# Softmax row sums of a small-head attention layer: GpSimd folds and VectorE with one transpose per group, in place of matmuls with ones

## The chip, the cores and the metric

One core of a Trainium2 chip runs the whole program. The metric is device time in microseconds (us), the median of several executions.

## The reference

The program is a decoder of four layers on x (8 sequences of 128 tokens, width 256), each layer a mixer, a cross block and a feed-forward block, each behind a layer norm and added to x. The change touches the mixer of layer 1 alone, an attention with 32 query heads of width 8, 8 key/value heads (one for four query heads), rotary embeddings and a causal mask:

```python
x = x + _L1_attn_ref(_layernorm(x, axis=-1), L1_attn_Wq, L1_attn_Wk, L1_attn_Wv, L1_attn_Wo)
# inside, for each sequence and each head h of 32, with kv head h // 4:
#   P = softmax(q_h @ k.T / sqrt(8) + causal mask)        (128 x 128)
#   y_h = P @ v                                           (128 x 8)
# and the 32 heads side by side times Wo
```

The kernel computes exp(score - row maximum) first, multiplies that by v, and divides by the row's sum of exponentials afterwards.

## The kernel before

All data of the stage lies in SBUF. The layer's name in the code is `l1a`; the cross block of layer 2 (`l2x`) has heads of the same size and runs through the same code, `heads`. It has a version on each engine: TensorE at L921, ScalarE near L1674, VectorE near L2358.

A **unit** `u` is four heads of one sequence: 128 queries x 4 x 128 keys, 64 units in all (UNITS). Its four jobs are:

- `("s", u)`: a mask matmul and a score matmul fill one PSUM bank (128 x 512). VectorE takes the negated row maxima (L2371), ScalarE writes four exponentials of 128 x 128 into a ring of eight slots in `work` at 12288 (L1697). The bank is free when the last of the four is written.
- `("t", u)`: TensorE transposes the four 128 x 128 blocks (L957) into a bank; ScalarE (even units, L1703) or VectorE (odd units, L2380) copies the bank into a ring of eight slots in `work` at 8192.
- `("pv", x)`, one for the four units of group `x`: TensorE multiplies by windows of v (16 matmuls) and then by windows of ones (16 matmuls), so that one bank holds the unnormalised outputs, heads times channels on the partitions and queries along the columns, and beside them the sums, in the same layout. VectorE inverts the sums (L2387) and multiplies (L2391) into XT. TensorE waits for the copies of the group's last two units.
- `("o", bp)`, for four groups: the output projection, then the residual add on VectorE (L2403) and the statistics for the next layer norm (L2040, L2043).

**The order** is a list written out by `heads_plan`, in rounds of three units. Every engine walks the same list and picks its own work. Round `r` holds the scores of units 3r to 3r+2, a `pv` if one is due (group x in round (4x+3)//3 + 2), the transposes of the round before, and an `o` if one is due. Engines run strictly in their own order.

**PSUM banks**: the function `banks` hands the eight banks to the jobs in the order of the lists, one after the other, round and round. On TensorE `begin` waits until the job that last had the bank has freed it. For a round's scores, TensorE takes all three banks before the first mask matmul:

```python
os = [begin(layer, "s", u) for u in units]
```

GpSimd does nothing in this stage but the two small square roots of the next layer norm (`roots`, L647 and L650, on halves of the sequences), which follow in its program directly on those of this layer. SyncE loads the next weights and starts the next context loads when the last job of `l1a` is full. The array C holds data of an earlier stage that is no longer read.

Of the kernel before, what the change touches and what calls it, by code (L numbers as in the profile page):

```python
# [6 lines left out]
P = 128  # L7
NB = 8
D = 256
# [146 lines left out]
def heads_plan(sums_at=None):  # L156


    l = []
    for r in range(ROUNDS + 5):  # L160
        l += [("s", u) for u in round_of(r)]
        if r == sums_at:
            l += [("ws",)]
        l += [("pv", x) for x in range(UNITS // 4) if (4 * x + 3) // 3 + 2 == r]
        l += [("t", u) for u in round_of(r - 1)]
        if sums_at is not None and r == ROUNDS + 1:
            l += [("qt", 0)]
        l += [("o", bp) for bp in range(4) if (16 * bp + 15) // 3 + 4 == r]
    return l
# [73 lines left out]
def build(nc, a, out):  # L243
# [3 lines left out]
    with ExitStack() as ctx:  # L247
# [70 lines left out]
        tables_ready, queries_out = sem("tables_ready"), Handoff("queries_out")  # L318
        halves_ready, steps_ready, rates_ready = sem("halves_ready"), sem("steps_ready"), sem("rates_ready")
        half_steps, turned, head_squares, head_roots = Handoff("half_steps"), Handoff("turned"), Handoff("head_squares"), Handoff("head_roots")  # L320
        sums_inverse, scaled_probs = Handoff("sums_inverse"), Handoff("scaled_probs")
        to_turn, key_normed, key_rooted = Handoff("to_turn"), Handoff("key_normed"), Handoff("key_rooted")
        key_squares, key_roots, scaled_keys, to_park = Handoff("key_squares"), Handoff("key_roots"), Handoff("scaled_keys"), Handoff("to_park")
# [143 lines left out]


        keys_beside = WA[:, 5200:5456]

        def l1a_k(g):

# [159 lines left out]
        def _(pool):  # L632
# [52 lines left out]
            for k, n in enumerate(("k", "ks")):  # L685
                for c in range(2):
                    nc.gpsimd.tensor_copy(r3(keys_beside[:, c * P + k * 64:c * P + k * 64 + 64], 8),
                                          W(WA, W_L1A, n, c * D, (c + 1) * D).rearrange("p (a r d) -> p a r d", r=4, d=8)[:, :, 0, :]).then_inc(tables_ready, 1)
            roots()
            roots()  # L690
            def turn(q, cos, sin):

# [155 lines left out]
        def _(pe):  # L848
# [72 lines left out]
            def heads(layer, wo, pad):  # L921

                kbd = r3(wk(0, 8 * N), N)
                for key in heads_plan(SUMS_AT if layer == "l2x" else None):
# [29 lines left out]
                    if key[0] == "t":  # L954
                        pe.wait_ge(*freed(J(layer, "s", key[1])))
                        for i in range(4):
                            ins = nc.tensor.transpose(o[:, i * P:(i + 1) * P],  # L957
                                                      wk(12288 + (key[1] % 8) * G + i * P, P), cst("ident"))
                        end(ins)
                    elif key[0] == "pv":  # L960

                        x = key[1]
                        pe.wait_ge(*freed(J(layer, "t", 4 * x + 2)))
                        pe.wait_ge(*freed(J(layer, "t", 4 * x + 3)))
                        for part in range(2):
                            for h in range(4):
                                for k in range(4):
                                    u = 4 * x + k
                                    window = v_windows[:, u * 32 + 24 - 8 * h:u * 32 + 56 - 8 * h] if part == 0 else ones_window[:, 24 - 8 * h:56 - 8 * h]
                                    ins = mm(o[32 * k:32 * k + 32, part * P:(part + 1) * P], window,  # L970
                                             wk(8192 + (u % 8) * G + h * P, P), h == 0, h == 3)
                        end(ins)
                    else:
                        bp = key[1]
                        for x in range(4):
                            pe.wait_ge(*freed(J(layer, "pv", 4 * bp + x)))
                        for i in range(2):
                            for c in range(2):
                                lo = (bp % 2) * G + (2 * i + c) * P
                                ins = mm(o[:, i * D:(i + 1) * D], XT[:, lo:lo + P],  # L980
                                         wo[:, c * D:(c + 1) * D], c == 0, c == 1)
                        end(ins)
# [539 lines left out]
        def _(act):  # L1522
# [151 lines left out]
            def heads(layer):  # L1674
                for key in heads_plan(SUMS_AT if layer == "l2x" else None):
# [16 lines left out]
                    if key[0] == "s":  # L1692
                        act.wait_ge(dve_to_act.sem, dve_to_act.next())
                        if u >= 8:
                            act.wait_ge(*full(J(layer, "t", u - 8)))
                        for h in range(4):
                            f(wk(12288 + (u % 8) * G + h * P, P), bank(j)[:, h * P:(h + 1) * P], ACT.Exp,  # L1697
                              bias=sm(704 + (u % 8) * 4 + h, 1)).then_inc(*act_step(*([j] if h == 3 else [])))
# [333 lines left out]
        def _(dve):  # L2032
# [317 lines left out]
            def hidden_evac(b):  # L2350
# [4 lines left out]
                    dve.wait_ge(*full(J("l2f", "o", b - 4)))  # L2355
                v.tensor_copy(XT[:, :].bitcast(BF16)[:, (b % 4) * 1024:(b % 4 + 1) * 1024], bank(j).bitcast(BF16)).then_inc(*dve_step(j))

            def heads(layer):  # L2358

                for key in heads_plan(SUMS_AT if layer == "l2x" else None):  # L2360
# [20 lines left out]
                    elif key[0] == "pv":  # L2381
                        x = key[1]
                        bp, lo = x // 4, (x // 4 % 2) * G + (x % 4) * P
                        j = J(layer, "pv", x)
                        dve.wait_ge(*full(j))
                        rs = wk(17920, P)
                        v.reciprocal(rs, bank(j)[:, P:2 * P]).then_inc(*dve_step())  # L2387
                        dve.wait_ge(*dve_last())
# [1 line left out]
                            dve.wait_ge(*full(J(layer, "o", bp - 2)))  # L2390
                        v.tensor_tensor(XT[:, lo:lo + P], bank(j, P, P), rs, ALU.mult).then_inc(*dve_step(j))  # L2391
                        dve.wait_ge(*dve_last())
                    elif key[0] == "ws":
                        j = J(layer, "ws")
                        dve.wait_ge(*full(j))
# [548 lines left out]
```

## Time and profile before

| | us |
|---|---|
| median of 3 runs | 1538.31 (1536.23 to 1540.87) |
| span of the profiled execution | 1538.9 |
| TensorE busy | 1388.0 (90%) |
| VectorE busy | 912.7 (59%) |
| ScalarE busy | 766.8 (50%) |
| GpSimd busy | 453.6 (29%) |
| `heads` of `l1a`, first score to last residual add | 406 to 521 |
| transposes L957, both layers | 67.1 |
| exponentials L1697, both layers | 137.7 |

Busy time is that of an engine's instructions without register, branch and semaphore work. PE is TensorE, DVE VectorE, ACT ScalarE, POOL GpSimd. An fp32 matmul leaves two records, and some records are missing: of three mask matmuls often only two are there, and such a row starts 0.2 us late. Times of the trace are counted from the start of the span.

### The profile page before, as it was taken

How to read it: one execution, taken by the hardware profiler on the slowest of the kernel's cores; microseconds unless marked ns; L12 is line 12 of the kernel's file. 1: busy time of each engine (PE TensorE's matmuls, PEld its weight loads, DVE VectorE, ACT ScalarE, POOL GpSimd, SP SyncE). 2: the span in 40 equal slices, each digit the busy share in tenths (PEclk: the TensorE clock that was granted, in tenths of full speed). 3: DMA queues.
4: the chain of work that ended last, by engine and by line, in shares of the span. 5: the costliest groups of instructions: out<-in, count | busy, mean ns of one | idle time of the engine just before them, and what ended most of it. 6: DMA issues, size and time to landing. Idle time of an engine off the chain costs nothing.

```text
span 1538.9 us, 25724 instructions
## 1 busy us (share of the span) xinstructions
PE 1388.0 (90%) x9822; PEld 880.0 (57%) x9840; DVE 912.7 (59%) x1665; ACT 766.8 (50%) x1847; POOL 453.6 (29%) x400
## 2 busy tenths in 40 slices
PE   7868999999899879999999989988996888888799
PEld 3534565555466545666666764654663545546636
DVE  6694322224578655645555787945787576575632
ACT  3362111111778567777776457448776453362230
POOL 3140000000000268886881000110924235314100
PEclk9888999999999999999999999998998788989989
DMA  8020211001200300000000100020001100000000
GB/s 255 14 96 1 67 49 44 1 0 63 102 2 2 125 0 7 8 8 7 8 8 1 76 23 1 1 82 1 3 2 71 56 0 3 3 1 3 29 1 28
DMA packets 21854, 48.12 MB, mean 31 GB/s; under 512 B 1506, under 2 KB 16995, under 8 KB 20580
## 3 DMA queue, kind: packets, MB, share of 16 engines
q1 hardware_dynamic: 21732, 46.47, 8.7%
q8 instruction: 79, 1.29, 0.4%
q14 instruction: 43, 0.35, 0.1%
HBM read 41.22 MB, written 5.24 MB: 30 GB/s over the span
## 4 chain that ended last, share of the span: by engine, by line
PE 67%; DVE 19%; ACT 6%; issue 4%; POOL 4%; DMA 0%; DVEq 0%; ACTq 0%; POOLq 0%
PE PS L862 48%; PE PS L1092 5%; DVE work L2568 4%; PE PS L1151 3%; PE PS L957 3%; PE PS L1392 2%; ACT work L1697 2%; PE PS L874 2%; PE PS L1189 2%; DVE small L2040 1%; PE PS L1421 1%; DVE work L2186 1%; DVE X L2547 1%; DVE work L2536 1%; POOL work L795 1%
## 5 line engine op out<-in xcount | busy, mean ns | idle before, releaser
L862 PE MATMUL PS<-XT,WB 128*128 128x512 f32 (+1 forms) x688 | 300.0, 594 | 5.1 <-DVE XT L2066 2.8
L862 PEld LDWEIGHTS PS<-XT,WB 128*128 128x128 f32 (+1 forms) x688 | 126.7, 190 | 149.1 <-issue 145.4
L1697 ACT ACTIVATE work<-PS,small 128x128 f32<-128x128 f32 x512 | 137.7, 416 | 45.2 <-DVE small L2371 45.2
L2261 DVE TENSOR_TENSOR work<-PS,work 128x512 f32<-128x512 f32 x48 | 33.1, 691 | 168.4 <-PE PS L862 168.4
L1625 ACT ACTIVATE work<-PS 128x512 f32<-128x512 f32 x48 | 28.7, 597 | 193.6 <-PE PS L862 193.6
L647 POOL TENSOR_SCALAR small<-small 128x4 f32<-128x4 f32 x22 | 5.0, 229 | 405.9 <-DVE small L2043 405.8
L2371 DVE TENSOR_REDUCE small<-PS 128x4 f32<-128x512 f32 x128 | 80.5, 684 | 41.2 <-PE PS L862 39.8
L862 PE MATMUL PS<-XT,WA 128*128 128x512 f32 (+2 forms) x224 | 97.7, 596 | 6.1 <-DVEq L2571 3.7
L2568 DVE SCALAR_TENSOR_TENSOR work<-PS,vec,work 128x508 f32<-128x508 f32 (+2 forms) x108 | 80.2, 742 | 14.4 <-DVE work L2568 7.2
L1092 PE MATMUL PS<-WB,work 128*128 128x256 f32 x384 | 86.9, 379 | 0.5 <-DVE work L2266 0.5
L1092 PEld LDWEIGHTS PS<-WB,work 128*128 128x128 f32 x384 | 72.8, 190 | 18.3 <-issue 7.7
L862 PE MATMUL PS<-WA,XT 128*128 128x256 f32 (+1 forms) x384 | 78.1, 362 | 3.3 <-DVE XT L2391 2.4
L862 PE MATMUL PS<-work,WA 128*32 128x128 f32 (+1 forms) x2072 | 75.5, 278 | 3.0 <-DVE work L2380 1.8
L862 PE MATMUL PS<-work 128*128 128x64 f32 (+4 forms) x368 | 73.8, 351 | 3.0 <-DVE work L2620 1.8
L862 PEld LDWEIGHTS PS<-work,WA 128*32 128x32 f32 (+1 forms) x2072 | 57.6, 111 | 32.5 <-issue 32.5
L862 PEld LDWEIGHTS PS<-WA,XT 128*128 128x128 f32 x384 | 67.5, 190 | 12.3 <-issue 4.5
L862 PEld LDWEIGHTS PS<-XT,WA 128*128 128x128 f32 (+2 forms) x224 | 39.0, 186 | 60.6 <-issue 50.1
L1544 ACT ACTIVATE XN<-X,small 128x256 f32<-128x256 f32 x44 | 24.0, 593 | 97.8 <-DVE small L2049 97.6
L874 PE MATMUL PS<-cst,XN 128*128 128x128 f32 x176 | 37.5, 372 | 35.9 <-DVE XN L2053 35.4
L957 PE MATMUL PS<-cst,work 128*128 128x128 f32 x512 | 67.1, 281 | 2.8 <-ACT work L1697 2.8
L862 PE MATMUL PS<-WB,C 128*128 128x256 f32 (+1 forms) x287 | 67.3, 379 | 0.2
L957 PEld LDWEIGHTS PS<-cst,work 128*128 128x128 f32 x512 | 56.2, 143 | 19.5 <-issue 19.5
(375 smaller groups left out, 2893.7 us busy)
## 6 DMA issues: line engine op xcount, KB each, us to landing
WB<-in_l0f SPq DMA_DIRECT2D x8, 768.0 KB, 7.6
WB<-in_l1x SPq DMA_DIRECT2D x1, 6144.0 KB, 18.2
WB<-in_l0f SPq DMA_DIRECT2D x32, 96.0 KB, 7.3
WB<-in_l2f SPq DMA_DIRECT2D x1, 3072.0 KB, 10.5
WA<-in_l3a SPq DMA_DIRECT2D x1, 2624.0 KB, 8.9
WB<-in_l3f SPq DMA_DIRECT2D x1, 2064.0 KB, 7.8
WA<-in_l1f SPq DMA_DIRECT2D x1, 2056.0 KB, 11.2
C<-in_ctx SPq DMA_DIRECT2D x2, 1024.0 KB, 7.0
```

Of the source, the lines that this page charges most:

```text
L862: mm = lambda o, l, r, s, e: nc.tensor.matmul(o, l, r, start=s, stop=e)
L874: ins = nc.tensor.transpose(o[:, i * P:(i + 1) * P], source[:, b * D + c * P:b * D + (c + 1) * P], cst("ident"))
L957: ins = nc.tensor.transpose(o[:, i * P:(i + 1) * P], wk(12288 + (key[1] % 8) * G + i * P, P), cst("ident"))
L1092: ins = nc.tensor.matmul(o[:, i * D:(i + 1) * D], l0f_h(x)[:, b * P:(b + 1) * P], quad(x // 3, "down")[:, x % 3 * D:(x % 3 + 1) * D], star ...
L1151: ins = nc.tensor.matmul(o[:, i * D:(i + 1) * D], l1x_q(t // 4, 2 * s_ + i)[:, r * P:(r + 1) * P], wk(8192 + (t // 4 % 2) * 1024 + r * D, ...
L1189: ins = nc.tensor.transpose(o[:, j * P:(j + 1) * P], l1x_p(x)[:, j * D + kc * P:j * D + (kc + 1) * P], cst("ident"))
L1392: more = lambda o, l, r, e: nc.tensor.matmul(o, l, r, start=False, stop=e, skip_group_check=True)
L1625: f(l0f_s(m)[:, g * G:(g + 1) * G], bank(j), ACT.Silu).then_inc(*act_step(j))
L1697: f(wk(12288 + (u % 8) * G + h * P, P), bank(j)[:, h * P:(h + 1) * P], ACT.Exp, bias=sm(704 + (u % 8) * 4 + h, 1)).then_inc(*act_step(*([j ...
L2261: v.tensor_tensor(l0f_h(m)[:, lo:lo + G], bank(j), l0f_s(m)[:, lo:lo + G], ALU.mult).then_inc(*dve_step(j))
L2371: v.tensor_reduce(sm(704 + (u % 8) * 4, 4), r3(bank(j), P), AX.X, ALU.max, negate=True).then_inc(*dve_step(dve_to_act))
L2568: v.scalar_tensor_tensor(d[:, :, k:P], p[:, :, 0:P - k], vec(taps[0], taps[1] + 3 - k), d[:, :, k:P], ALU.mult, ALU.add).then_inc(*dve_ste ...
```

## The change

- `heads_plan` gets a job `("rb", x)` for each group in `l1a`, one round behind the group's `pv` and ahead of a `pv` in the same round.
- GpSimd folds each unit's exponentials: the 128 columns of each of four blocks to 64 (`fold_once`), then to 32 (`fold_twice`, a ring of eight slots). The first fold of unit u waits until the unit's exponentials are written, the second for the first and, from unit 8 on, until VectorE has passed the group that used the slots.
- VectorE, at a group's `pv`: `inverse_of(x)` reduces 4 x 128 folded columns to 16 sums, inverts them, and spreads each over 8 columns (128 x 128). Then it copies the `pv` bank to XT. At `rb` it multiplies XT by the `rb` bank.
- TensorE: `pv` has only the 16 matmuls with v in this layer; `rb` is one transpose of the spread inverses into a bank. The output projection waits for `rb` in place of `pv`.
- ScalarE, from unit 8 on, waits before a unit's exponentials also for the first fold of the unit eight before, whose slot it overwrites.
- `l2x` keeps its matmuls with ones and its order.

```diff
--- before.py
+++ after.py
@@ -161,6 +161,8 @@
         l += [("s", u) for u in round_of(r)]
         if r == sums_at:
             l += [("ws",)]
+        if sums_at is None:
+            l += [("rb", x) for x in range(UNITS // 4) if (4 * x + 3) // 3 + 3 == r]
         l += [("pv", x) for x in range(UNITS // 4) if (4 * x + 3) // 3 + 2 == r]
         l += [("t", u) for u in round_of(r - 1)]
         if sums_at is not None and r == ROUNDS + 1:
@@ -318,6 +320,7 @@
         tables_ready, queries_out = sem("tables_ready"), Handoff("queries_out")
         halves_ready, steps_ready, rates_ready = sem("halves_ready"), sem("steps_ready"), sem("rates_ready")
         half_steps, turned, head_squares, head_roots = Handoff("half_steps"), Handoff("turned"), Handoff("head_squares"), Handoff("head_roots")
+        folded_once, folded_twice, inverse_sums = sem("folded_once"), sem("folded_twice"), sem("inverse_sums")
         sums_inverse, scaled_probs = Handoff("sums_inverse"), Handoff("scaled_probs")
         to_turn, key_normed, key_rooted = Handoff("to_turn"), Handoff("key_normed"), Handoff("key_rooted")
         key_squares, key_roots, scaled_keys, to_park = Handoff("key_squares"), Handoff("key_roots"), Handoff("scaled_keys"), Handoff("to_park")
@@ -467,6 +470,18 @@
 
 
         keys_beside = WA[:, 5200:5456]
+
+        def fold_once(u):
+
+            return C[:, (u % 2) * D:(u % 2 + 1) * D]
+
+        def fold_twice(u, n=1):
+
+            return C[:, 512 + (u % 8) * P:512 + (u % 8 + n) * P]
+
+        def inverse_spread(x):
+
+            return wk(17920 + (x % 2) * P, P)
 
         def l1a_k(g):
 
@@ -687,6 +702,15 @@
                     nc.gpsimd.tensor_copy(r3(keys_beside[:, c * P + k * 64:c * P + k * 64 + 64], 8),
                                           W(WA, W_L1A, n, c * D, (c + 1) * D).rearrange("p (a r d) -> p a r d", r=4, d=8)[:, :, 0, :]).then_inc(tables_ready, 1)
             roots()
+            for u in range(UNITS):
+                halves = r3(wk(12288 + (u % 8) * G, G), P)
+                pool.wait_ge(*freed(job_of[("l1a", "s", u)]))
+                nc.gpsimd.tensor_tensor(r3(fold_once(u), 64), halves[:, :, 0:64], halves[:, :, 64:P], ALU.add).then_inc(folded_once, 1)
+                pool.wait_ge(folded_once, u + 1)
+                if u >= 8:
+                    pool.wait_ge(inverse_sums, (u - 8) // 4 + 1)
+                once = r3(fold_once(u), 64)
+                nc.gpsimd.tensor_tensor(r3(fold_twice(u), 32), once[:, :, 0:32], once[:, :, 32:64], ALU.add).then_inc(folded_twice, 1)
             roots()
             def turn(q, cos, sin):
 
@@ -962,7 +986,7 @@
                         x = key[1]
                         pe.wait_ge(*freed(J(layer, "t", 4 * x + 2)))
                         pe.wait_ge(*freed(J(layer, "t", 4 * x + 3)))
-                        for part in range(2):
+                        for part in range(1 if layer == "l1a" else 2):
                             for h in range(4):
                                 for k in range(4):
                                     u = 4 * x + k
@@ -970,10 +994,13 @@
                                     ins = mm(o[32 * k:32 * k + 32, part * P:(part + 1) * P], window,
                                              wk(8192 + (u % 8) * G + h * P, P), h == 0, h == 3)
                         end(ins)
+                    elif key[0] == "rb":
+                        pe.wait_ge(inverse_sums, key[1] + 1)
+                        end(nc.tensor.transpose(o[:, 0:P], inverse_spread(key[1]), cst("ident")))
                     else:
                         bp = key[1]
                         for x in range(4):
-                            pe.wait_ge(*freed(J(layer, "pv", 4 * bp + x)))
+                            pe.wait_ge(*freed(J(layer, "rb" if layer == "l1a" else "pv", 4 * bp + x)))
                         for i in range(2):
                             for c in range(2):
                                 lo = (bp % 2) * G + (2 * i + c) * P
@@ -1693,6 +1720,8 @@
                         act.wait_ge(dve_to_act.sem, dve_to_act.next())
                         if u >= 8:
                             act.wait_ge(*full(J(layer, "t", u - 8)))
+                            if layer == "l1a":
+                                act.wait_ge(folded_once, u - 7)
                         for h in range(4):
                             f(wk(12288 + (u % 8) * G + h * P, P), bank(j)[:, h * P:(h + 1) * P], ACT.Exp,
                               bias=sm(704 + (u % 8) * 4 + h, 1)).then_inc(*act_step(*([j] if h == 3 else [])))
@@ -2355,6 +2384,18 @@
                     dve.wait_ge(*full(J("l2f", "o", b - 4)))
                 v.tensor_copy(XT[:, :].bitcast(BF16)[:, (b % 4) * 1024:(b % 4 + 1) * 1024], bank(j).bitcast(BF16)).then_inc(*dve_step(j))
 
+            def inverse_of(x):
+
+                sums, inverse = C[:, 1536:1552], C[:, 1552:1568]
+                dve.wait_ge(folded_twice, 4 * x + 4)
+                v.tensor_reduce(sums, r3(fold_twice(4 * x, 4), 32), AX.X, ALU.add).then_inc(*dve_step())
+                dve.wait_ge(*dve_last())
+                v.reciprocal(inverse, sums).then_inc(*dve_step())
+                dve.wait_ge(*dve_last())
+                if x >= 2:
+                    dve.wait_ge(*full(J("l1a", "rb", x - 2)))
+                v.tensor_copy(r3(inverse_spread(x), 8), inverse.unsqueeze(2).to_broadcast([P, 16, 8])).then_inc(inverse_sums, 1)
+
             def heads(layer):
 
                 for key in heads_plan(SUMS_AT if layer == "l2x" else None):
@@ -2382,7 +2423,14 @@
                         x = key[1]
                         bp, lo = x // 4, (x // 4 % 2) * G + (x % 4) * P
                         j = J(layer, "pv", x)
+                        if layer == "l1a":
+                            inverse_of(x)
                         dve.wait_ge(*full(j))
+                        if layer == "l1a":
+                            if bp >= 2:
+                                dve.wait_ge(*full(J(layer, "o", bp - 2)))
+                            v.tensor_copy(XT[:, lo:lo + P], bank(j, P, P)).then_inc(*dve_step(j))
+                            continue
                         rs = wk(17920, P)
                         v.reciprocal(rs, bank(j)[:, P:2 * P]).then_inc(*dve_step())
                         dve.wait_ge(*dve_last())
@@ -2390,6 +2438,13 @@
                             dve.wait_ge(*full(J(layer, "o", bp - 2)))
                         v.tensor_tensor(XT[:, lo:lo + P], bank(j, P, P), rs, ALU.mult).then_inc(*dve_step(j))
                         dve.wait_ge(*dve_last())
+                    elif key[0] == "rb":
+                        x = key[1]
+                        bp, lo = x // 4, (x // 4 % 2) * G + (x % 4) * P
+                        j = J(layer, "rb", x)
+                        dve.wait_ge(*full(j))
+                        dve.wait_ge(*freed(J(layer, "pv", x)))
+                        v.tensor_tensor(XT[:, lo:lo + P], XT[:, lo:lo + P], bank(j, P, P), ALU.mult).then_inc(*dve_step(j))
                     elif key[0] == "ws":
                         j = J(layer, "ws")
                         dve.wait_ge(*full(j))
```

## Rows read from the trace of the kernel before

**Rows 1.** The page, part 1: busy time, share of the span, instructions.
```profile
PE 1388.0 (90%) x9822; PEld 880.0 (57%) x9840; DVE 912.7 (59%) x1665; ACT 766.8 (50%) x1847; POOL 453.6 (29%) x400
```

**Rows 2.** Busy time by stretch: stretch, length, each engine's, granted clock, DMA share, GB/s.
```profile
420.00:440.00 20.00, 19.26 (x317) 13.38 (x313) 16.07 (x27) 16.48 (x58) 0.00 (x0) 1.00 0.01 2
```

**Rows 3.** Timeline in `l1a`: start us, length us, engine, line, operation, [idle before, releaser].
```profile
418.46 1.13 PE L862 MATMUL PS<-work,XN 32*128 32x512 f32 x6
...
447.65 1.13 PE L862 MATMUL PS<-work,XN 32*128 32x512 f32 x6
...
454.43 1.13 PE L862 MATMUL PS<-work,XN 32*128 32x512 f32 x6
...
457.61 0.81 PE L862 MATMUL PS<-causalb,identb 128*128 128x512 bf16 x3 [0.58 <-ACT work L1697]
458.34 1.13 PE L862 MATMUL PS<-work,XN 32*128 32x512 f32 x6
...
459.41 1.95 PE L862 MATMUL PS<-work,WA 128*32 128x128 f32 x64
459.50 1.89 DVE L2371 TENSOR_REDUCE small<-PS 128x4 f32<-128x512 f32 x3 [0.83 <-PE PS L862]
460.23 3.21 ACT L1697 ACTIVATE work<-PS,small 128x128 f32<-128x128 f32 x12 [0.21 <-DVE small L2371]
...
461.29 1.53 PE L957 MATMUL PS<-cst,work 128*128 128x128 f32 x12
461.43 0.96 DVE L2387 RECIPROCAL work<-PS 128x128 f32<-128x128 f32 x1
462.42 0.29 DVE L2391 TENSOR_TENSOR XT<-PS,work 128x128 f32<-128x128 f32 x1
...
463.40 1.14 PE L862 MATMUL PS<-work,XN 32*128 32x512 f32 x6
...
504.31 1.13 PE L862 MATMUL PS<-work,XN 32*128 32x512 f32 x6
```

**Rows 4.** Timeline in `l2x`, around its round 7.
```profile
1074.96 0.81 PE L862 MATMUL PS<-WA,identb 128*128 128x512 bf16 x3 [0.57 <-ACT work L1697]
...
1077.59 3.21 ACT L1697 ACTIVATE work<-PS,small 128x128 f32<-128x128 f32 x12 [0.21 <-DVE small L2371]
...
1080.94 0.81 PE L862 MATMUL PS<-WA,identb 128*128 128x512 bf16 x3 [0.45 <-ACT work L1697]
```

**Rows 5.** VectorE's groups by line and form: busy us, mean ns; L2793: min/median/max ns.
```profile
L2380 DVE COPY work<-PS 128x512 f32<-128x512 f32 x64 | 42.1, 685 | 2.4 <-PE PS L957 1.2 <-DVE XT L2391 0.2
...
L2503 DVE RECIPROCAL small<-small 128x4 f32<-128x4 f32 x32 | 5.7, 178 | 52.6 <-ACT work L1745 29.4 <-ACT XN L1745 23.2
...
L2793 DVE TENSOR_REDUCE small<-work x2: 676/681/686, 1454.5 to 1455.2; 128x4 f32<-128x512 f32 x2
```

**Rows 6.** GpSimd's adds: L703 by group, and L697's min/median/max ns.
```profile
L703 POOL TENSOR_TENSOR work<-work,WB 128x512 f32<-128x512 f32 x37 | 47.6, 1288 | 2.9
...
L697 POOL TENSOR_TENSOR WB<-work,small x37: 1259/1263/1604, 533.0 to 803.6; 64x512 f32<-64x512 f32 x37
```

**Rows 7.** Timeline in `l1x`: a VectorE operation inside a GpSimd operation.
```profile
599.13 1.26 POOL L696 TENSOR_TENSOR WB<-work,small 64x512 f32<-64x512 f32 x1
599.58 0.83 DVE L2496 SCALAR_TENSOR_TENSOR small<-small 128x2 f32<-128x2 f32 x1
```

**Rows 8.** Timeline in `l1a`: the last unit's score and the last output projection.
```profile
508.94 1.12 PE L862 MATMUL PS<-work,XN 32*128 32x512 f32 x2
...
518.36 1.97 PE L862 MATMUL PS<-WA,XT 128*128 128x256 f32 x8 [1.49 <-DVE XT L2391]
```

**Rows 9.** Three stretches, with the columns of rows 2.
```profile
410.00:415.00 5.00, 3.25 (x21) 1.79 (x21) 2.02 (x4) 5.00 (x21) 0.00 (x0) 1.00 0.01 3
1045.00:1050.00 5.00, 2.30 (x12) 0.92 (x10) 1.29 (x3) 5.00 (x16) 0.00 (x0) 0.90 0.01 3
1050.00:1055.00 5.00, 5.00 (x20) 3.21 (x20) 2.61 (x5) 3.85 (x14) 0.00 (x0) 0.50 0.00 0
```

## The prediction

> **What bounds the kernel now.** I read the page first: TensorE is busy for 90% of the span and every other engine far less [rows 1]. An average says little about one stage, so the next view is the busy time in a stretch of the stage that the change touches: TensorE 19.3 of 20 us, ScalarE 16.5, VectorE 16.1, GpSimd nothing, at full clock [rows 2]. So TensorE sets the pace there, but ScalarE is close behind. The third view is the order of instructions in a few rounds [rows 3]. A round is: three mask matmuls, the three score matmuls (start `s`), the probability-times-value matmuls of a group of four units if one is due (`pv`, 1.95 us, 64 records), twelve transposes (`t`, 1.53 us). VectorE takes three maxima (1.89 us) that start 1.16 us behind the scores; ScalarE's twelve exponentials start 1.89 us behind the scores (458.34 to 460.23) and last 3.21 us. A round with a `pv` lasts 5.06 us (scores at 458.34 and 463.40). The round before it has none and lasts 3.91 us (454.43 to 458.34), and there TensorE waited 0.58 us for an exponential before the next masks. What it waits for is a PSUM bank. Scores, transposes and `pv` results take the eight banks in turn, each job the bank of the job eight before it, and all three score banks of a round are taken before its first mask. That wait decides this case.
>
> **What leaves TensorE.** In this layer the half of `pv` with the ones window goes: half of 1.95 us, 0.98 us, 16 times. One transpose of 128 columns comes for each (a twelfth of 1.53 us, 0.13 us). TensorE gets 0.85 us shorter per group, 13.6 us in all [rows 3].
>
> **What the new bank job does.** The new transpose `rb` takes a bank of its own. I counted the plan's jobs. Before, a round with `pv` is seven jobs (s s s pv t t t), so the third score of the next round takes the bank that the second score of this round left: its exponentials must be over, which they are before TensorE gets there. With `rb` and `pv` in a round it is eight jobs, and each score takes the bank of the same score one round earlier: the next round can't start until the third, last score is through its exponentials. Walked through with the new list, the round that starts next waits on the third score at rounds 5, 6, 9, 10, 13, 14, 15, 17, 18, 20 (ten times), on the second at 4, 7, 8, 11, 12, 16, 19 (seven), on the first at 21. The sixteen more jobs are two full turns, so all later layers keep their banks.
>
> The loop that then sets the pace has no `pv` and no transposes in it: masks (0.73 us to the scores, 457.61 to 458.34), 1.89 us to the exponentials, 3.21 us to the end of the third, 0.14 us back to TensorE (exponentials from 1077.59 for 3.21 us, masks at 1080.94 [rows 4]): 0.73 + 1.89 + 3.21 + 0.14 = 5.97 us. Waiting on the second score it is a third of the exponentials less, 4.90 us; on the first 3.83 (3.91 is what the round shown takes). The trace has one such eight-job round already: in the second small-head layer round 7 holds an extra one-matmul job, the eighth. From mask to mask it took 5.98 us (1074.96 to 1080.94), and TensorE idled 0.45 us for an exponential though that round's own work was longer than in the changed kernel [rows 4]. So the loop is as read.
>
> **The sum of the rounds.** From the scores of round 3 (418.46) to those of round 20 (504.31) are 17 rounds, 85.9 us now. After: 10 x 5.97 + 7 x 4.90 = 94.0 us, so +8.1. Is TensorE short enough everywhere? Its longest round, with the output projection too, is round 9: now 6.78 us (447.65 to 454.43), then 5.93, just below the loop. The step from round 20 to 21 waits on the first score only and is TensorE's own, 4.63 now, 0.85 less: -0.8. Rounds 0 to 3 don't change.
>
> **VectorE.** Per group it loses the reciprocal of 128 columns (0.96) and a multiply (0.29) [rows 3]. It gains a reduce from SBUF of 512 columns (0.68, the same form at another line) [rows 5], a reciprocal of 16 columns (between 0.18 for 4 and 0.96 for 128; near the former, 0.25) [rows 3, 5], a spread over 128 columns (between nothing and the 0.29 of the multiply of 128 columns, two inputs; I take 0.22), a copy out of PSUM (0.28) and the multiply (0.29): 1.72 for 1.25, +0.5 us a group. With maxima 1.89, up to two copies 1.37 [rows 5] and handoffs an eight-job round costs it 5.2 us of 5.97: covered. The order matters more than the sum. The group's inverse stands behind the round's maxima and in front of the copies that TensorE's next `pv` needs: those end 7.0 us after the masks, and the next maxima are due at 7.9 (5.97 + 0.73 + 1.16). Round 9 has the residual add and statistics as well and comes about 0.3 us late: +0.3. If this cover were gone, every tenth of VectorE lateness would come out ten times.
>
> **GpSimd.** Per unit a fold of 256 columns and one of 128. No such fold is in the trace; the same engine's add over 512 columns takes 1.27 to 1.29 us, another 512-column form 1.26, at worst 1.60 [rows 6]. By columns the pair (384 of 512) costs 0.97 us, at worst 1.2, with handoffs of some 0.1 each (estimated, L703's idle of 2.9 us over 37) about 1.2 to 1.4 us. The 17 rounds give it 94.0 us for 51 units, 1.84 each. It is hidden. ScalarE's new wait (fold of the unit eight before) has over two rounds of slack; behind it are queued the exponentials that everything waits for. The fold's wait for the group's inverse holds GpSimd until VectorE has passed it; behind it only folds are queued, and those of a group are wanted more than a round after its last exponential. GpSimd's square roots for the next layer norm are queued behind the folds too; they are wanted after the last residual add, some 10 us behind the last exponential.
> The two engines can also hold each other up: a VectorE operation on two columns took 0.83 us where it began inside a GpSimd operation, ending 0.02 us behind it [rows 7]. The Trainium skill (SBUF — State Buffer, "SBUF: two separate sides") says why: the second port pair is an exclusive lock, held for a whole instruction by either engine, and a VectorE operation of one SBUF input takes it in a 2-port mode. By that rule the spread, if it runs in that mode, could wait for one fold, up to 0.65 us. The row shows the lock for two inputs only, so I leave it out of the sum; by the rule VectorE's copies would end at 7.65 in place of 7.0, still ahead of 7.9.
>
> **The tail.** From the last score (508.94) to the output projection (518.36) are 9.4 us [rows 8]. After: maxima and exponential as now (to 3.0), transposes with one `rb` and the shorter `pv` ahead (to 4.4), VectorE with the inverse, copies and multiply ahead of the last copy (to 5.4), last `pv` (0.98) to 6.5, copy out of PSUM 6.8, multiply 7.1 (its transpose has come by then): 7.2 us. -2.2.
>
> Total: +8.1 - 0.8 + 0.3 - 2.2 = **+5.4 us**. On the profiled execution's span of 1538.9 us that gives 1544.3; the median is 1538.3, 0.6 less, so I forecast **1543.7 us**.
>
> **Rivals.**
> *A, faster: the bank wait doesn't decide.* If the exponentials of a round ended before TensorE comes round again, what TensorE loses would be saved until ScalarE binds: ScalarE is busy 82% of the time now [rows 2], so a 5.06 us round can shrink to about 4.4 us. 14 rounds with `pv` save 0.65 each, 9.1, and the tail 2.2: 1527 us. It decides if the loop of 5.97 us is below 4.4, and nothing shortens its 1.89 + 3.21; against it stands the eight-job round of rows 4. 0.10.
> *B, GpSimd binds.* It decides above 1.84 us per unit. Were a fold to cost what the 512-column add costs, whatever its width (2 x 1.27 and 0.16 of handoffs, 2.7 us), 64 units would last 173 us against 118 at 1.84: some 1599 us; a pair at 2.0 us, from overhead on its short rows of 32 and 64 elements, gives +10, 1554. For it: no narrow two-input fold is in the trace. Against: the engine starts with 2.5 rounds in hand. 0.08.
> *C, the clock falls.* In the new rounds TensorE works 4.3 of 5.97 us. In the stretch 410 to 415 it worked 3.25 of 5 us and kept the full 2.4 GHz; after it had worked only 2.30 of the 5 us from 1045 to 1050, the granted clock was 0.50 in the next five, which is 1.2 GHz [rows 9]. TensorE's 4.3 us of a round would be 8.6 then, 2.6 over the loop; three such rounds give +8, 1552 us. The Trainium skill (TensorE: Matmul & The Clock Gate, "A second HAM failure mode: psum-queue depth-cycling") describes just this, idling between groups of matmuls as PSUM banks cycle makes the clock swing; the rows so far don't show it at gaps of 1.6 us. 0.06.
> *D, the loops bind but less*, the tail and the shorter rounds giving back all: 1539. 0.06.
>
> **How the numbers follow.** My forecast has 0.70, with its own range of 1541 to 1548 for the reciprocal's, spread's and lock's bounds (0.1 us late in each of ten rounds is 1 us) and the times' own spread. The range over cases, 1536 to 1553, leaves out A and most of B. A measurement here tells about 0.3%, 4.6 us, from no change. Faster: A, 0.10. Slower: two thirds of the forecast, B and C: 0.61. Same: the rest, 0.29.
>
> **What would show it.** Right: waits of TensorE for the exponentials of L1697 ahead of the masks some 15 times, about 1 to 1.6 us each; scores 5.97 us apart into the ten rounds named and 4.9 into the seven; TensorE busy near 75% in the stage, GpSimd near 60%; `pv` 32 records in 0.98 us. Wrong: score distances near 4.4 (A), exponentials waiting for a GpSimd line (B), clock under 1.00 between 420 and 510 (C), or maxima that start late behind the inverse, which would make it slower than the sum.

## Result and profile after

The changed kernel takes 1550.8 us in the median of 20 runs, the kernel before 1540.3 us on the same chips: a ratio on record of 1.0061 (that of the two medians is 1.0068), 95% interval 1.0045 to 1.0077. It is slower, by 7 to 12 us. The forecast was slower by 5.4, so the direction is right and the size is below the interval. Put on the 1538.3 us that the forecast started from, the ratio gives 1547.7 us, inside the 1541 to 1548 of the forecast's own case; the 1550.8 us itself lies only in the wider range, 1536 to 1553.

The page of the changed kernel, part 1 (busy time, share of the span, instructions), answers to rows 1, and the row by stretch to rows 2 (in order TensorE, its weight loads, VectorE, ScalarE, GpSimd, clock):

```profile
PE 1383.6 (89%) x9326; PEld 870.1 (56%) x9344; DVE 915.7 (59%) x1713; ACT 766.3 (50%) x1847; POOL 530.2 (34%) x528
```

```profile
420.00:440.00 20.00, 15.08 (x170) 9.10 (x174) 13.87 (x30) 13.92 (x48) 13.93 (x24) 1.00 0.00 1
```

In the stage no engine is the bound any more: TensorE fell from 19.3 to 15.1 of 20 us, but ScalarE and VectorE are less busy too. GpSimd went from nothing to 13.9. The clock stayed full. The stage's time went to waiting, and the view of who waited for whom, from 405 us to just beyond the stage's end, names the waits of TensorE; first the kernel before, then the changed one (total us, times, longest):

```profile
PE PS L862 <- ACT work L1697: 3.1, 5, 1.0
```

```profile
PE PS L886 <- ACT work L1726: 17.7, 13, 1.6
...
PE PS L886 <- DVE work L2397: 3.2, 4, 0.8
```

The second line of the changed kernel names VectorE's spread, but in the code TensorE's waits ahead of these masks are for score banks alone. The spread ended within 0.2 us of the second unit's exponentials (into round 4: 420.04 and some 419.87 us), and the view takes what came last. Both lines are the one bank wait, 17 times in all; e3 bears it out, since those rounds move too when only the bank wait is moved.

The timeline of two rounds of the changed kernel, to be read beside rows 3 (start us, length us, engine, line, operation, idle before and releaser):

```profile
426.23 0.59 PE L886 MATMUL PS<-causalb,identb 128*128 128x512 bf16 x2 [1.58 <-ACT work L1726]
...
426.76 1.13 PE L886 MATMUL PS<-work,XN 32*128 32x512 f32 x6
...
427.82 0.33 PE L999 MATMUL PS<-cst,work 128*128 128x128 f32 x1
427.92 1.89 DVE L2412 TENSOR_REDUCE small<-PS 128x4 f32<-128x512 f32 x3 [1.35 <-PE PS L886]
...
428.08 1.08 PE L886 MATMUL PS<-work,WA 128*32 128x128 f32 x32
428.64 3.20 ACT L1726 ACTIVATE work<-PS,small 128x128 f32<-128x128 f32 x12 [2.28 <-DVE small L2412]
...
429.09 1.53 PE L981 MATMUL PS<-cst,work 128*128 128x128 f32 x12
429.72 0.28 DVE L2447 TENSOR_TENSOR XT<-XT,PS 128x128 f32<-128x128 f32 x1
...
429.92 0.68 DVE L2391 TENSOR_REDUCE C<-C 128x16 f32<-128x512 f32 x1
430.62 0.25 DVE L2393 RECIPROCAL C<-C 128x16 f32<-128x16 f32 x1
...
430.91 0.30 DVE L2397 COPY work<-C 128x128 f32<-128x128 f32 x1
...
431.13 0.28 DVE L2432 COPY XT<-PS 128x128 f32<-128x128 f32 x1
...
432.20 0.59 PE L886 MATMUL PS<-causalb,identb 128*128 128x512 bf16 x2 [1.58 <-ACT work L1726]
```

TensorE ends its transposes at 430.6 and then stands until the third unit's exponentials are over (428.64 + 3.20 = 431.84). The round lasts 5.97 us. Products with v now take 1.08 us and leave 32 records for 64 (the transposes start 1.01 us behind their start, 1.88 before).

The distances of the scores, read from the timeline from round 3 on, into rounds 4 to 21:

| into round | 4 | 5 | 6 | 7 | 8 | 9 | 10 | 11 | 12 | 13 | 14 | 15 | 16 | 17 | 18 | 19 | 20 | 21 |
|---|---|---|---|---|---|---|---|---|---|---|---|---|---|---|---|---|---|---|
| before | 5.05 | 5.06 | 5.05 | 3.92 | 5.05 | 5.06 | 6.78 | 3.91 | 5.06 | 5.05 | 5.06 | 4.94 | 5.06 | 5.05 | 5.06 | 3.91 | 6.78 | 4.63 |
| changed | 4.94 | 5.97 | 5.96 | 4.94 | 4.94 | 5.96 | 6.18 | 4.93 | 4.94 | 5.97 | 5.97 | 5.97 | 4.93 | 5.97 | 5.97 | 4.94 | 5.96 | 4.01 |

From the scores of round 3 to the start of the last output projection the stage takes 99.9 us before and 106.3 us now: +6.4 us.

### The profile page after: what moved, and what is told of

Its sections match the earlier page's. It is cut to its first block, busy times and chain, and to the rows that moved or that the text cites. A ratio compares the mean times of both kernels' runs of the same rounds, so it can differ in the third digit from the quotient of the medians.

```text
span 1546.6 us, 25008 instructions
## 1 busy us (share of the span) xinstructions
PE 1383.6 (89%) x9326; PEld 870.1 (56%) x9344; DVE 915.7 (59%) x1713; ACT 766.3 (50%) x1847; POOL 530.2 (34%) x528
## 4 chain that ended last, share of the span: by engine, by line
PE 63%; DVE 20%; ACT 7%; issue 5%; POOL 4%; DMA 0%; DVEq 0%; ACTq 0%; POOLq 0%
PE PS L886 46%; PE PS L1119 5%; DVE work L2623 4%; ACT work L1726 3%; PE PS L1178 3%; PE PS L1419 2%; PE PS L981 2%; PE PS L1216 2%; PE PS L898 1%; DVE small L2069 1%; DVE small L2412 1%; PE PS L1448 1%; DVE work L2215 1%; DVE X L2602 1%; DVE work L2591 1%
## 5 line engine op out<-in xcount | busy, mean ns | idle before, releaser
L886 PE MATMUL PS<-XT,WA 128*128 128x512 f32 (+2 forms) x224 | 98.3, 615 | 4.5 <-DVE XT L2095 2.3
L886 PEld LDWEIGHTS PS<-WA,XT 128*128 128x128 f32 x384 | 69.1, 196 | 11.2 <-issue 3.3
L697 POOL COPY WB<-WB 128x1536 f32<-128x1536 f32 x8 | 11.7, 1466 | 184.7 <-PE PS L886 184.7
L1178 PE MATMUL PS<-work 128*128 128x256 f32 x256 | 67.7, 396 | 0.0
```

What stands on the lines that cost most here:

```text
L886: mm = lambda o, l, r, s, e: nc.tensor.matmul(o, l, r, start=s, stop=e)
L1178: ins = nc.tensor.matmul(o[:, i * D:(i + 1) * D], l1x_q(t // 4, 2 * s_ + i)[:, r * P:(r + 1) * P], wk(8192 + (t // 4 % 2) * 1024 + r * D, ...
```

## Experiments

All are compared with the kernel before, run on the same chip. "Stage" is that stretch, from the scores of round 3 to the last output projection.

**e0: the changed kernel once more**

> The changed kernel itself once more, for a second profile of it beside the one at hand. In the first profile the stage from the scores of round 3 to the last output projection takes 106.3 us for 99.9 before, +6.4 us, but the whole time is 0.6% or some 9 us longer. Theory (the bank wait is the whole cause, the rest is the granted clock of later stages, which differs from run to run): ratio 1.004 to 1.008, the stage again 106.3 us, and the later stages differ from the first profile by some us without a pattern. Rival (the change makes a later stage slower in itself): the same later stretch is longer than before in both profiles, by the same 3 us.

Ratio 1.0055 (1.0034 to 1.0075). The stage took 106.4 us, every round as in the table within 0.05 us, while the span of this profile was 1539.8 us for 1546.6. The stretches that no edit touches differ between the profiles:

| us | before | changed | e0 | e6 |
|---|---|---|---|---|
| start to the first score of `l1a` | 406.4 | 403.9 | 403.7 | 402.2 |
| stage | 99.9 | 106.3 | 106.4 | 106.4 |
| stage's end to the first score of `l2x` | 521.3 | 524.2 | 521.9 | 521.1 |
| after the last score of `l2x` | 389.9 | 391.9 | 386.4 | 390.6 |

No later stretch is longer by the same 3 us in the first two profiles of the changed kernel: between the stage and `l2x` it is 2.9 us and 0.6 us more than before, after `l2x` 2.0 us more and 3.5 us less. So the rival falls as it was put. What these stretches follow is TensorE's granted clock. Between the stage and `l2x` it was 0.99, 0.97, 0.98 and 0.98 in the order of the table, and after `l2x` 0.90, 0.88, 0.91 and 0.90: the longest stretch has the lowest clock each time. In the stage it was 1.00. One profile's span says nothing about 5 us; a stage's length does.

**e1: the kernel before with an empty bank job**

```diff
@@ heads_plan
+        if sums_at is None:
+            l += [("rb", x) for x in range(UNITS // 4) if (4 * x + 3) // 3 + 3 == r]
@@ TensorE
+                    elif key[0] == "rb":
+                        end(nc.tensor.transpose(o[:, 0:P], cst("ident"), cst("ident")))
@@ VectorE
+                    elif key[0] == "rb":
+                        j = J(layer, "rb", key[1])
+                        dve.wait_ge(*full(j))
+                        v.tensor_copy(C[:, 0:1], bank(j)[:, 0:1]).then_inc(*dve_step(j))
```

> The kernel before, its matmuls with ones kept, with one more bank job per group in l1a in the place of rb: one transpose of a constant and a copy of one column, nothing waits for the result. Bank-wait theory: the third-score loop of 5.97 us sets the eight-job rounds. Into rounds 5, 6, 9, 13, 14, 15, 17, 18: 5.97 us; into 10 and 20, TensorE's own 6.9 and 6.8; into 4, 8, 12, 16: 5.06; into 7, 11, 19: 4.90. From the scores of round 3 to those of round 20 96.4 us for 85.9 now, in all some +11 us, ratio 1.007. Rival (what costs is the added work of VectorE and GpSimd, the bank job only its own 0.13 us): +2 us, ratio 1.001 to 1.002.

Ratio 1.0074 (1.0048 to 1.0100). The rounds into 5, 6, 9, 13, 14, 15, 17, 18 took 5.96 or 5.97 us, into 7, 11 and 19 4.94, into 4, 8, 12, 16 5.06, into 10 and 20 7.04 and 6.78; from round 3 to round 20 96.6 us. The stage took 111.1 us, +11.2 where I expected some +11. TensorE ahead of the scores of round 5:

```profile
430.92 0.59 PE L864 MATMUL PS<-causalb,identb 128*128 128x512 bf16 x2 [0.70 <-ACT work L1701]
```

With no fold, no inverse and nobody who needs its result, the job makes the same 5.97 us, with a wait of 0.7 us in a round in which TensorE still has its full work. The bank job alone is enough.

**e2: the changed kernel without the bank job**

```diff
@@ TensorE, pv: the transpose goes into the free half of the pv bank
+                        if layer == "l1a":
+                            pe.wait_ge(inverse_sums, x + 1)
+                            ins = nc.tensor.transpose(o[:, P:2 * P], inverse_spread(x), cst("ident"))
                         end(ins)
@@ VectorE, t: behind the last copy of the round that holds the group's last unit
+                        if layer == "l1a" and u == round_of(u // 3)[-1]:
+                            for x in range(UNITS // 4):
+                                if (4 * x + 3) // 3 == u // 3:
+                                    inverse_of(x)
@@ VectorE, pv
-                            v.tensor_copy(XT[:, lo:lo + P], bank(j, P, P)).then_inc(*dve_step(j))
+                            v.tensor_copy(XT[:, lo:lo + P], bank(j, P, P)).then_inc(*dve_step())
+                            dve.wait_ge(*dve_last())
+                            v.tensor_tensor(XT[:, lo:lo + P], XT[:, lo:lo + P], bank(j)[:, P:2 * P], ALU.mult).then_inc(*dve_step(j))
```

The `rb` job goes from the plan and from every engine, and the waits for `rb` become waits for `pv`.

> The changed kernel without the bank job: the transpose of the inverses goes into columns 128 to 255 of the group's own pv bank, behind the products with v, and VectorE forms the inverse one round earlier, behind its copies of that round. All of the new work of GpSimd and VectorE stays. Bank-wait theory: no round waits for a third score; rounds with pv go to the second-score loop of 4.90 us or less for 5.06 before, those without stay at 3.9: some 4 us less than before over the rounds and 2 at the tail, ratio to before 0.996. Rival (VectorE's chain of reduce, reciprocal, spread, copy and multiply is what costs): rounds with pv stay near 5.3 us, ratio 1.000 to 1.004.

Ratio 0.9987 (0.9968 to 1.0006): the slowdown is gone. The stage took 97.6 us, 8.7 less than in the changed kernel. But of the eleven steps out of rounds with a `pv` and no output projection, only those into 5, 9, 13 and 17 reached the second-score loop's length (4.94 or 4.95); the other seven took 5.03 to 5.77. In those seven the maxima start 0.09 to 0.86 us later than the usual 1.16 us behind the scores, and each step is 4.94 us and that lateness, to 0.03 us. VectorE is then still in the inverse (into 16, the latest, in the residual add and the statistics too), and into 6, 14 and 18 its spread started inside a fold and took 0.69 us for 0.23. So both named causes exist: the bank wait is what the change lost by, and with that gone VectorE's chain holds most of what was left to win. I had put it at 0.996.

**e3: each bank waited for ahead of its own mask**

```diff
-                        os = [begin(layer, "s", u) for u in units]
-                        for u, o in zip(units, os):
+                        os = []
+                        for u in units:
+                            o = begin(layer, "s", u)
+                            os.append(o)
                             b = u // 8
```

> The changed kernel, but TensorE waits for each score bank just ahead of its own mask matmul and not for all three ahead of the first. The bank jobs and all work stay. Bank-wait theory: the loop loses two of the three masks, about 0.4 us (0.73 to 0.34 from the last wait to the scores): 5.55 us for the third score, 4.5 for the second, 17 rounds less 0.4 each: 6.6 us less than the changed kernel, ratio to before 1.001 to 1.002. The same code runs in l2x, where it gives 0.4 us in some five rounds. Rival (the rounds are paced by VectorE or GpSimd): no gain in l1a, ratio to before 1.005 to 1.006.

Ratio 0.9986 (0.9970 to 1.0002). The bank jobs are all there, and the changed kernel is no slower than the one before. The 5.97 us rounds took 5.47 or 5.48, those of 4.94 took 4.43 or 4.44 (4.62 into round 4); rounds 9 and 19, with a `pv` and the output projection on TensorE, took 6.18 and 5.91 for 6.18 and 5.96. The stage is 98.9 us, 7.4 less than in the changed kernel. On TensorE the two waits now stand between the masks:

```profile
432.44 0.39 PE L886 MATMUL PS<-causalb,identb 128*128 128x512 bf16 x1 [0.25 <-ACT work L1728]
433.47 0.39 PE L886 MATMUL PS<-causalb,identb 128*128 128x512 bf16 x1 [0.65 <-ACT work L1728]
```

The ratio is below what I expected in part because `l2x` runs the same code: from its first score to its last it took 106.2 us for 109.3, where I had counted some five rounds of 0.4 us.

**e4: both edits together, and e9, the same on another chip**

> The two edits together on the changed kernel: the inverses' transpose in the pv bank (no rb job) and each score bank waited for just ahead of its own mask. Bank-wait theory with VectorE next in line (in e2 the maxima came up to 0.9 us late behind the inverse's chain): the second-score loop falls to 4.43, so VectorE, with 17.3 us of work in four rounds, and its order set the pace; rounds with pv 4.5 to 4.9 us, from the scores of round 3 to those of round 20 79 to 82 us for 85.9 before, ratio to before 0.993 to 0.995. If VectorE's chain alone set the rounds of e2, the second edit gives nothing in l1a: 85 us again, ratio 0.998.

> e4 once more, beside e7 and e5 on one chip: the version that is faster than both kernels. The stages give -6.2 us in l1a and -3.1 in l2x, ratio 0.994; the first measurement gave 0.991. I expect 0.990 to 0.994, and faster than e5 by the 4.6 us of its stage, 0.3%.

Ratios 0.9912 (0.9887 to 0.9937) and 0.9937 (0.9916 to 0.9958): faster than both kernels. The stage took 93.7 us in both, 6.2 less than before, `l2x` 105.6 and 105.9. From round 3 to round 20 it is 81.5 us, inside the 79 to 82 expected; the first ratio is below the 0.993 to 0.995 expected. Out of rounds with a `pv` and no output projection the steps are 4.47 or 4.48 us and 5.09 to 5.31. Against the kernel before with the wait alone moved (e5 and e8 below, on the same two chips) the stage is 4.6 us shorter, but the time is only 1.7 and 0.2 us lower, where I expected 4.6. The mean granted clock of e9's runs was 0.952 to 0.954 and that of e8's 0.954 to 0.962; how much of the missing gain that is, no run here tells.

**e7: e4 with a short reduce**

```diff
-                v.tensor_reduce(sums, r3(fold_twice(4 * x, 4), 32), AX.X, ALU.add).then_inc(*dve_step())
+                v.tensor_reduce(sums, r3(fold_twice(4 * x, 4), 32)[:, :, 0:4], AX.X, ALU.add).then_inc(*dve_step())
```

> e4 with VectorE's reduce over 4 of each head's 32 folded columns: 64 in place of 512 columns, the other columns of the sums are left out and the outputs of the layer are not the reference's. In e4 the rounds alternate between 4.47 us (the bank wait) and 5.1 to 5.2 us. Theory: the longer ones are VectorE's, whose maxima are late behind the inverse; 0.5 us less work per group brings those eleven rounds to 4.5 to 4.7 and the distance from round 3 to round 20 from 81.5 to 76 or 77 us, ratio to before 0.987 to 0.989. Rival (these rounds are TensorE's or the banks'): 81.5 us again, ratio 0.991.

Ratio 0.9898 (0.9865 to 0.9931); 78.6 us from round 3 to round 20, 2.8 less than e4, where I expected 4.5 to 5.5. Into rounds 6, 14 and 18 it fell from 5.1 to 4.43 or 4.44; into 8, 12 and 16 only from 5.17, 5.17 and 5.30 to 4.95, 4.95 and 5.08; into 4 from 5.16 to 5.13. So VectorE's work ahead of the maxima does set several of these rounds. It holds the rest too, by the timeline. Into 6, 14 and 18 the maxima now start on time; into 4, 8, 12 and 16 they are still 0.70, 0.53, 0.53 and 0.68 us late, and each step is 4.43 us and that lateness, to 0.03 us. Ahead of them the spread, which took 0.23 us in these rounds of e4, now started inside a fold of GpSimd and took 0.46 to 0.75. Into round 8, where the scores start at 431.38 and the maxima were due at 432.54:

```profile
432.31 0.75 POOL L706 TENSOR_TENSOR C<-work 128x256 f32<-128x256 f32 x1
...
432.67 0.48 DVE L2397 COPY work<-C 128x128 f32<-128x128 f32 x1
...
433.07 1.27 DVE L2412 TENSOR_REDUCE small<-PS 128x4 f32<-128x512 f32 x2
```

The reduce gave 0.47 us and the spread took 0.25 of it back. The time is 8.7 us below e9's on the same chip, with four runs and six, where the stage gives 3.3; that difference is open.

**e5: the kernel before with only the edit of e3, and e8, the same on another chip**

> The kernel before, with each score bank waited for just ahead of its own mask; nothing else. Bank-wait theory: the rounds with pv are TensorE's own 5.06 us and don't move; those without pv (into 7, 11 and 19) wait on the first score and lose 0.4 us of 3.91 at most; in l2x as many and its round 8. Together 2 to 3.5 us, ratio 0.998. If the place of the wait mattered in every round, as in e3, it would be 17 x 0.4 in each of the two layers, some 14 us, ratio 0.991.

> e5 once more, on another chip. Its two changed stages were 1.6 and 3.1 us shorter in the profile (ratio 0.997) while its time was 0.993 of before. Theory: the difference is the granted clock of the untouched stages, which moves each profile by some us: ratio 0.993 to 0.998, and the untouched stretches of this profile are again within the spread of all profiles. Rival: the edit gives something beyond its stages, and those stretches are shorter in both profiles.

Ratios 0.9929 (0.9906 to 0.9952) and 0.9939 (0.9917 to 0.9960). The profiles agree with the theory round by round: those with `pv` stay at 5.05 or 5.06 us, those into 7, 11 and 19 fall from 3.91 to 3.40. The stage is 98.3 and 98.4 us, `l2x` 106.2 in both, together 4.6 us less, 0.3%. The time fell by 0.6 to 0.7%. The untouched stretches are 403.5, 520.2 and 389.8 us in e5's profile, in sum 4.0 us less than before, but about the same as in e0's and e6's; in e8's they are 401.8, 523.7 and 392.9 us, in sum 0.7 us more than before. So the rival's second half doesn't hold: a gain of some 5 to 6 us beyond the stages is in both times, but not in the profiles of both. The clock doesn't account for it: the median of the runs' mean granted clocks is 0.959 for 0.958 in e5 and 0.957 for 0.957 in e8. I can't say where it comes from.

**e6: the changed kernel with tiny folds**

```diff
-                nc.gpsimd.tensor_tensor(r3(fold_once(u), 64), halves[:, :, 0:64], halves[:, :, 64:P], ALU.add).then_inc(folded_once, 1)
+                nc.gpsimd.tensor_tensor(fold_once(u)[:, 0:4], wk(12288 + (u % 8) * G, 4), wk(12288 + (u % 8) * G + 64, 4), ALU.add).then_inc(folded_once, 1)
```

(and `fold_twice` over 4 columns in the same way)

> The changed kernel with GpSimd's folds over 4 columns in place of 256 and 128; the same instructions, waits and semaphores, the sums are left out and the outputs of the layer are not the reference's. Bank-wait theory: GpSimd's 1.2 us per unit are hidden, so the rounds stay at 5.97 and 4.94 us and only the last group's inverse can come earlier: 0 to 0.5 us less than the changed kernel, ratio to before 1.005 to 1.006. Rival (GpSimd's pace or its hold on VectorE's spread costs): the rounds get shorter, ratio 1.003 or less.

Ratio 1.0045 (1.0024 to 1.0065), stage 106.4 us, the rounds at 5.98 and 4.94 as with whole folds. GpSimd's groups, first the changed kernel, then e6:

```profile
L708 POOL TENSOR_TENSOR C<-work 128x256 f32<-128x256 f32 x64 | 47.2, 738 | 44.5 <-ACT work L1726 44.5
L713 POOL TENSOR_TENSOR C<-C 128x128 f32<-128x128 f32 x64 | 29.3, 457 | 20.6 <-DVE work L2397 16.4
```

```profile
L713 POOL TENSOR_TENSOR C<-C 128x4 f32<-128x4 f32 x64 | 12.7, 199 | 30.4 <-DVE work L2397 26.5
L708 POOL TENSOR_TENSOR C<-work 128x4 f32<-128x4 f32 x64 | 12.7, 199 | 83.8 <-ACT work L1726 83.7
```

51 us less work on GpSimd change nothing in the stage. It is hidden, as forecast.

## Why the prediction was right, step by step

- **TensorE's share.** Forecast 0.98 us less and 0.13 more per group; the start of the transposes behind the scores moved from 2.95 us (rows 3) to 2.33 in a round with `rb`, 0.62 less where the forecast gives 0.85. The products are the size forecast (1.08 us); `rb` holds the next products back by 0.26 us (427.82 to 428.08), not by 0.13. It cost nothing in most rounds, since TensorE then waits for the bank, but it set round 9.
- **The bank wait.** Forecast: loops of 5.97 and 4.90 us, the third score waited for into ten named rounds, the second into seven. Measured: 5.96 or 5.97 into nine of the ten, 4.93 or 4.94 into all seven. e1 shows that the job alone brings it, e2 and e3 that taking it away or moving its wait takes the loss away, with GpSimd's and VectorE's new work in place. In e3 3.1 of the 4.0 us that the two stages are shorter than before come from `l2x`; in `l1a` the stage is 1.0 us shorter than before.
- **The sum of the rounds.** Forecast 94.0 us, and 0.3 for round 9; measured 94.4, where round 9 took 6.18 for 5.97. The number is right, the reason given for the 0.3 is not. The maxima behind round 9 start 1.15 us behind the scores, on time in spite of the residual add and statistics (454.74 and 455.89), and TensorE doesn't wait ahead of those scores. Round 9 is TensorE's own: the forecast had it at 5.93 us with 0.85 less, and with the 0.62 less that was measured, 6.78 us becomes 6.16. That the two slips nearly cancel is luck.
- **VectorE.** The parts came as sized: reduce 0.68, reciprocal 0.25, spread 0.23 (226 ns median), copy 0.28, multiply 0.28. That it is covered held in the changed kernel; how thin the cover is, e2 shows. I weighed it there only against the loop of 5.97, and expected too much of e2 for that reason.
- **GpSimd.** I took 0.97 to 1.2 us a pair; it is 0.74 + 0.46 = 1.20, the upper bound. By columns the folds of 256 and 128 would be 0.65 and 0.32. Still under the 1.84 us that a unit has, and hidden (e6).
- **The last step and the tail.** From round 20 to 21 4.01 us, -0.6 for -0.8 forecast. From the last score to the output projection 7.85 us where I worked out 7.2, so -1.6 for -2.2: the mis-sized term. The row is

```profile
516.22 1.08 PE L886 MATMUL PS<-work,WA 128*32 128x128 f32 x32 [0.53 <-DVE work L2421]
```

VectorE's two copies ahead of this next to last `pv` (514.79 to 516.06) stand behind the inverse and the copy out of PSUM, and TensorE waits 0.53 us for them; I had counted that for the last `pv` only. So the last transposes end 5.0 us behind the score (519.30) and not 4.4, and the rest of the tail keeps that lateness.
- **The total.** Stage +6.4 for +5.4. The time moved by 9.4 us in the first comparison, by 0.55% (8.5 us) in e0 and 0.45% (6.9 us) in e6, which share the stage to 0.1 us. The intervals reach down to 6.9, 5.2 and 3.7 us: in e0 and e6 the stage can be all of it, and the first comparison's ends 0.5 us above it. The profiles show stretches that no edit touches moving by up to 7.6 us from one to the next. In the 20 runs of the changed kernel the time goes with the mean granted clock, from 1540 us at 0.961 to 1555 to 1559 us at 0.944. Whether the change itself lowers the clock of other stages, and costs 2 us that way, isn't shown.
- **The lock between VectorE and GpSimd.** In the changed kernel the spread took 226 ns in the median and 303 at most: it mostly fell between folds, and ten times GpSimd stood still until it was over, since its second fold waits for that inverse. In e4 it is 381 in the mean, and the timeline has it inside a fold:

```profile
443.06 0.74 POOL L706 TENSOR_TENSOR C<-work 128x256 f32<-128x256 f32 x1
...
443.16 0.72 DVE L2397 COPY work<-C 128x128 f32<-128x128 f32 x1
```

The copy of one SBUF input takes 0.72 us in place of 0.23 and ends 0.08 us behind the fold. This is what the Trainium skill says (SBUF — State Buffer, "SBUF: two separate sides"), that a VectorE operation in a 2-port mode and a GpSimd operation shut each other out for a whole instruction. The maxima, which read PSUM, aren't held up beside folds (0.68 us each in the mean of e4's stage, as before). By that rule the trace agrees, and leaving it out of the sum was right for the changed kernel only because the folds lay elsewhere.
- **The rivals.** A would have needed rounds near 4.4: none came below 4.93 until round 21. B falls with e6. C falls with the clock of 1.00 from 415 to 523 us. There TensorE was idle for up to 1.6 us a round; the Trainium skill (TensorE: Matmul & The Clock Gate, "A second HAM failure mode: psum-queue depth-cycling") has the clock swing when matmul groups idle as PSUM banks cycle, which this stage at 75% busy doesn't show.

## What to carry to other kernels

A job that takes its turn in a ring of buffers costs more than its own time: it moves every later job's partner by one, and the engine that had slack may now wait for the newest user instead of an older one. Count jobs per round against the ring before adding one; if a bank has free columns, put the new result there, and wait for each buffer at its own use, not for all of a round ahead of the first. When the bound engine gets shorter, compare the whole loop through the other engines with its new length, since that loop may be just below the old one (here 4.94 us under 5.06). Any lateness inside that loop is then paid in full, as VectorE's maxima show in e2 and e7.

## What the runs showed of the hardware that I had not expected

- GpSimd's two-input fp32 adds cost more per column when narrow: 4 columns 0.20 us, 128 columns (four rows of 32) 0.46, 256 columns (four rows of 64) 0.74, against 1.26 to 1.29 us for 512 columns in another stage (rows 6).
- The three score matmuls on different 32-row groups run side by side: three take 1.13 us (six records, rows 3) and one alone 1.12 us (two records, rows 8). The maxima start 1.16 us behind the scores in both cases (458.34 and 459.50; 508.94 and 510.10 in the kernel before).
- Executions with the same stage, round for round, differ by 7 us in the span, in stretches that were not edited and whose granted clock differs by 0.01 to 0.03; and moving one wait in the kernel before (e5, e8) changed the time by twice what the edited stages show. That second point stays open.
